# Attention rows staged in DRAM per batch: aligned 160-key loads, 32-row score matmuls, a values product by columns

## What is computed

```
# layer 0: a per-batch 32x32 mixing matrix, then 8 experts (hidden 128), the best 2 of 8 for each row
x = x + experts0(einsum('bct,bcd->bdt', x, w[conditions]))

# layer 1: paged attention with a window of 128 keys, 8 query heads over 4 key/value groups of 32
q, k, v = project(x); q, k = rope(rms(q)), rope(rms(k))
k_blocks[blk, :, off, :] = k        # the 32 new rows of each batch go into blocks of 16 rows
v_blocks[blk, :, off, :] = v        # (tables of different batches share blocks)
k_all, v_all = k_blocks[block_tables], v_blocks[block_tables]
scores = q @ k_all * SCALE, masked to  pos - 128 < kpos <= pos
o = softmax(scores) @ v_all @ Wo

# then 2 experts (hidden 1024), the best 1 of 2 for each row
x = x + experts1(o)
```

## Time and profile before

| | us |
|---|---|
| median of 3 runs | 1221.78 (1213.56 to 1230.88) |
| the profiled execution | 1226.37 |
| its span, first to last instruction | 1224.6 |
| PE busy | 945.7 (77%) |
| DVE busy | 721.4 (59%) |
| POOL busy | 559.1 (46%) |
| ACT busy | 535.9 (44%) |

### The profile page before, as it was taken

The page is one execution under the profiler, slowest core; times in us unless marked ns, Lnnn a source line. Parts: engine busy times, 40 slices in busy tenths (PEclk is TensorE's granted clock), DMA queues, the critical chain, the costliest instruction groups (busy, mean ns, idle before and its releaser), DMA issues.

```text
span 1224.6 us, 21749 instructions
## 1 busy us (share of the span) xinstructions
PE 945.7 (77%) x4475; PEld 698.1 (57%) x4476; DVE 721.4 (59%) x2742; ACT 535.9 (44%) x1733; POOL 559.1 (46%) x558
## 2 busy tenths in 40 slices
PE   1896600789993766639988888888886999999995
PEld 1895400556662322218866677666774666767664
DVE  4225670344443899968978788878884444444442
ACT  0231000122221433329978787878783433333331
POOL 0001775050003777546777777777762122222221
PEclk9999999999997988968999999999997999999998
DMA  6766224874336644312222222222221111111110
GB/s 167 272 209 178 106 102 173 314 232 130 120 119 242 182 139 141 107 45 66 68 69 73 63 70 73 67 70 70 70 75 47 38 51 52 48 47 43 50 36 26
DMA packets 93174, 130.04 MB, mean 106 GB/s; under 512 B 28729, under 2 KB 77419, under 8 KB 91808
## 3 DMA queue, kind: packets, MB, share of 16 engines
q0 software_dynamic: 33872, 68.94, 18.9%
q1 hardware_dynamic: 44688, 42.02, 10.8%
q10 hardware_dynamic: 14576, 18.65, 5.0%
HBM read 98.37 MB, written 55.38 MB: 126 GB/s over the span
## 4 chain that ended last, share of the span: by engine, by line
PE 42%; issue 19%; POOL 19%; DMA 9%; DVE 8%; DVEq 1%; ACT 1%; SPq 0%; POOLq 0%; ACTq 0%
POOL kvring L417 12%; PE bank L839 9%; PE bank L851 9%; POOL slots_in L421 7%; PE bank L723 6%; PE bank L652 3%; DMA kvring<-written_blocks,read_i 2%; DMA work<-in_x 2%; PE bank L715 2%; PE bank L860 2%; PE bank L663 2%; DMA work<-slots_in 1%; DVE work L1153 1%; PE bank L731 1%; PE bank L770 1%
## 5 line engine op out<-in xcount | busy, mean ns | idle before, releaser
L421 POOL DMA_INDIRECT slots_in<-rows,slot_i x96 | 98.6, 1027 | 152.0 <-DVE slot_i L980 102.9
L417 POOL DMA_INDIRECT kvring<-in_cache,read_i x128 | 137.4, 1073 | 49.9 <-issue 36.0
L417 POOL DMA_INDIRECT kvring<-written_blocks,read_i x128 | 137.9, 1077 | 41.4 <-issue 40.8
L770 PE MATMUL bank<-work,kvring 88*128 88x256 f32 x512 | 136.0, 388 | 0.9 <-issue 0.8
L417 POOL DMA_INDIRECT work<-slots_out,slot_i x64 | 72.4, 1132 | 126.7 <-DMA slots_out<-work 102.4
L839 PE MATMUL bank<-experts,work 128*128 x264 | 126.4, 601 | 0.6 <-ACT work L621 0.6
L851 PE MATMUL bank<-experts,work 128*128 x528 | 124.9, 379 | 1.8 <-DVE work L1252 1.8
L851 PEld LDWEIGHTS bank<-experts,work 128*128 128x128 f32 x528 | 100.1, 190 | 43.2 <-issue 32.9
L421 POOL DMA_INDIRECT out_x<-work x33 | 33.2, 1007 | 191.2 <-DVE work L1264 178.4
L582 ACT ACTIVATE work<-work 128x176 f32<-128x176 f32 x256 | 110.3, 433 | 7.3 <-DVE work L1205 5.6
L1247 DVE TENSOR_TENSOR work<-bank,work 128x512 f32<-128x512 f32 x66 | 45.7, 692 | 106.4 <-ACT work L629 106.4
(11 more groups left out here) (235 smaller groups left out, 2016.2 us busy)
## 6 DMA issues: line engine op xcount, KB each, us to landing
slots_in<-work ACTq DMA_DIRECT2D x8, 1152.0 KB, 5.1
work<-slots_in SPq DMA_DIRECT2D x72, 128.0 KB, 2.1
slots_out<-work SPq DMA_DIRECT2D x72, 128.0 KB, 1.7
work<-in_x SPq DMA_DIRECT2D x64, 128.0 KB, 2.4
written_blocks<-kvring POOLq DMA_DIRECT2D x3, 2048.0 KB, 7.6
slots_in<-fill ACTq DMA_DIRECT2D x1, 4257.0 KB, 17.6
work<-slots_in SPq DMA_DIRECT2D x33, 129.0 KB, 2.6
x_rows<-work SPq DMA_DIRECT2D x32, 128.0 KB, 2.5
```

The source lines that it names most:

```text
L417: pool.indirect_dma_start(dst, None, src, bass.IndirectOffsetOnAxis(ap=index, axis=0), **kw).then_inc(done, 16)
L421: pool.indirect_dma_start(dst, bass.IndirectOffsetOnAxis(ap=index, axis=0), src, None, **kw).then_inc(done, 16)
L770: mm = pe.matmul(bank[6 + q // 2 % 2][:, (q % 2) * 256:(q % 2) * 256 + 256], kv[q][:, r * 256 + KW:r * 256 + 2 * KW], pt[q % 2][:, r * 256 ...
```

## The change

A DRAM buffer `kv_rows` (16 units of 8 batches, 8 x 176 rows each) holds for each batch its 11 blocks in order. POOL fills it in two rounds: in stages 2 and 3 with blocks of the cache (a gather of 88 blocks of 16 KB into SBUF, then a scatter of them to DRAM, for each unit), and from the start of attention with overwritten blocks over them. The block numbers for that go from DVE's `blocks_i` to DRAM by four DMAs of POOL, and come back turned, by four DMAs of SP, as `read_i`. In attention SP reads the batch's first row offset (0 to 15) into a register and loads exactly NK = 160 keys from there with one plain DMA into one of GB = 8 buffers. The mask becomes the same shape for all batches, but for keys before the start. Scores are multiplied by group: four matmuls with 32 rows contracted (partitions 32g on), 64 columns held and 160 keys streamed, into two banks. The values product has eight matmuls, 80 rows contracted, 32 columns held, 64 streamed, each writing its own 32 partitions. Queries come by one POOL copy for each tile, and the copy of the turned probabilities moves from DVE to ACT, that of the keys from ACT to DVE.

```diff
 @@ SP, between stage 1 and stage 2
+            sp.wait_ge(s4_list, 64)
+            for w in range(4):
+                sp.dma_start(read_i[:, w * NU:w * NU + NU], block_list[w].rearrange("(u c) -> c u", u=NU),
+                             allow_slow_non_contiguous=True).then_inc(s4_index, 16)
             sp.wait_ge(s_sc0, 16 * 2 * NT)
 @@ SP, attention
+            stage3_drained(sp)
+            for b in range(B):
+                u, j = b // GB, b % GB
+                if j == 0:
+                    sp.wait_ge(s4_rows[u % 2], 16 * (NU // 2 + u // 2 + 1))
+                wait(sp, s4_pv, b - GB + 1)
+                first = nc.s_assert_within(sp.value_load(first_i[0:1, b:b + 1]), 0, BLK - 1,
+                sp.dma_start(kv[j], kv_rows[u][bass.ds(first + j * ROWS_B, NK), :].rearrange(
+                    "(k r) f -> k (r f)", r=2)).then_inc(s4_in[j], 16)
 @@ POOL, after the block copies
             pool.wait_ge(s_idx, 1)
-            for b in range(RING):
-                gather(kv[b], cache_pairs, read_i[:, b:b + 1], s4_in[b], NPHYS * 8 - 1)
+            for w in range(4):
+                pool.dma_start(block_list[w].rearrange("(b k) -> b k", b=B), blocks_i[:, w * NR:w * NR + NR]).then_inc(s4_list, 16)
+            pool.wait_ge(s4_index, 64)
+            for u in range(PRE2 + 1):
+                if u < PRE2:
+                    wait(pool, s2_d, u * N0 // (PRE2 + 1))
+                    stage_cache(u)
+                if u:
+                    write_rows(u - 1)
 @@ POOL, stage 3, for each tile i
+                    u, phase = PRE2 + i // 4, i % 4
+                    if u < NU and phase == 0:
+                        stage_cache(u)
+                    if u < NU and phase == 3:
+                        write_rows(u)
 @@ POOL, attention
-                    gather(kv[b % RING], cache_pairs, read_i[:, b:b + 1], s4_in[b % RING], NPHYS * 8 - 1)
-                gather(kv[c0 % RING], copies_pairs, read_i[:, B + c0:B + c0 + 1], s4_in[c0 % RING], NE * B * 8 - 1)
+            stage_copies(0)
+            for tile in range(2):
+                queries(tile)
+            write_copies(0)
+            stage_copies(1)
+            write_copies(1)
+            for s in range(B + 16):
+                u, tile = s // GB + 2, s // BT + 1
+                if s % GB == 0 and u < NU:
+                    stage_copies(u)
+                if s % GB == 3 and u < NU:
+                    write_copies(u)
+                if s % BT == 0 and 2 <= tile < NT:
+                    queries(tile)
 @@ PE, attention: scores
-                        mm = pe.matmul(bank[2 + q % 2][:, g * NK:g * NK + NK],
-                                       qbd[q // 4 % 2][:, (q % 4) * 256 + g * P:(q % 4) * 256 + g * P + P], kt[q % 2],
+                    for g in range(G):
+                        p0 = HD * g
+                        mm = pe.matmul(sbank[set_][g // 2][64 * (g % 2):64 * (g % 2) + 64, 0:NK],
+                                       qb[t][p0:p0 + HD, q % 4 * 64:q % 4 * 64 + 64],
+                                       kt[q // 2 % 2][p0:p0 + HD, (q % 2) * NK:(q % 2) * NK + NK], start=True, stop=True)
 @@ PE, attention: values
-                        mm = pe.matmul(bank[6 + q // 2 % 2][:, (q % 2) * 256:(q % 2) * 256 + 256],
-                                       kv[q][:, r * 256 + KW:r * 256 + 2 * KW], pt[q % 2][:, r * 256:r * 256 + 256],
+                        for g in range(G):
+                            p0 = HD * g
+                            mm = pe.matmul(vbank[t][p0:p0 + HD, 0:D].rearrange("p (h b t) -> p b h t", h=2, b=BT)[:, q % 4, :, :],
+                                           kv[q][:, r * 256 + KW + p0:r * 256 + KW + p0 + HD],
+                                           pt[q % 2][:, r * 256 + 64 * g:r * 256 + 64 * g + 64], start=(r == 0), stop=(r == 1))
 @@ ACT, attention (DVE loses its copy of the turned probabilities)
+                    act.activation(pt[q], tbank[0:KR, :], ACT.Copy).then_inc(s4_tpc, 1)
+                    act.activation(ot[t], vbank[t][:, 0:D], ACT.Copy).then_inc(s4_oc, 1)
+                    act.activation(col(rows, tile * RW, D), vbank[t][:, D:2 * D], ACT.Copy).then_inc(s4_wc, 1)
                         act.activation(pr[q][:, g * NK:g * NK + NK], sc[q][:, g * NK:g * NK + NK], ACT.Exp,
-                    act.activation(kt[q], bank[q][:, 0:NK], ACT.Copy).then_inc(s4_ktc, 1)
-                    act.activation(dist[q], c("keypos"), ACT.Abs, bias=col(delta, st.s + 2)).then_inc(s4_di, 1)
```

368 lines of the change are left out of this document (182 added, 186 removed).

## The result

The changed kernel took 1617.26 us (median of 4 runs, 1614.03 to 1622.21), the kernel before 1223.66 beside it: a ratio of 1.323, with a 95% interval of 1.313 to 1.333. The forecast was 1295 with a range to 1380. The side was right, and the size was missed by more than 300 us.

What follows compares the result with a forecast made beforehand. The prediction took POOL to bound attention before, PE stage 2, and POOL's cycle the middle of stage 3. It summed +57 + 18 + 10 - 12 = +73 on 1226.4 us, less 4.6, to 1295 us, range 1210 to 1380.

Steps and rivals of the forecast that it cites:

- POOL never rests: Attention before: POOL's instructions and issue gaps fill 324 of 325 us, a pace of 2.92 us a batch.
- Part 1: Way to stage 2: SP's first load waits for POOL's stores, at 265 us (250 to 275); +57 us (+40 to +80).
- POOL pays some 12 us of the same kind: Stage 2: 16 transfers of 1.44 MB running through it cost some 12 us, within the +57.
- Part 2: Stage 3: 16 more transfers in POOL's list ahead of gathers DVE waits on; +18 us (+5 to +60).
- four buffers hide that, or they don't: Stage 3: later landing of small gathers and scatters is hidden by four buffers, or costs 16 x 2 to 4 us.
- Part 3: Attention's start: gather, scatter and load follow each other, 15 us in place of 4; +10 us (+5 to +16).
- Part 4: Attention's batch: 2.83 us against 2.92 by columns streamed, -12 us over 128 batches; chance 0.42.
- PE sets the batch: Attention: PE's passes sum to 2.83 us a batch, against 2.0 each for ACT and DVE.
- lands in 2.5 us: Attention: SP's load of 160 keys takes some 2.5 us, hidden while a batch takes over 2.2 us.
- Rival 1: Attention: passes on strips run beside each other, about 2.4 us a batch, -67 us, total 1240 us; chance 0.27.
- the round trip decides: Within Rival 1: scores, masks, exponentials, copy, then values take some 2.8 us, giving about 2.4 us a batch.
- Rival 3: Attention: short passes cost more than their columns, batch 3.23 to 3.63 us, total 1347 to 1398 us; chance 0.23.

Runs made afterwards that it cites:

- e17: e13 unchanged, run again together with e16; 1235.92 us, ratio 1.016 to the kernel before.
- e5: e3 with the masking of scores moved first in each step of DVE's attention loop; 1357.87 us.
- e1: Changed kernel with only two of 16 units filled in the first (cache) round, so most batches read another batch's keys; 1490.14 us.
- e4: Changed kernel with scores and values multiplied in whole-array forms, including products nobody asked for; 1612.84 us.
- e11: Changed kernel with the mask first on DVE and scores and values in e4's whole-array forms, output not attention's result; 1617.85 us.
- e2: Changed kernel with the four loads of block numbers issued by POOL and not SP; 1586.44 us.
- the combined kernel: The kernel of e10, all four repairs on the changed kernel; 1297.22 us as it was, 1271.9 us with 96 rows (e18).
- e15: e10 with `PRE2 = 16`, so the whole first round lies beside stage 2; 1339.8 us where the kernel before took 1320.49.
- e6: e3 with one more matmul per batch into an unused part of a bank, read by nobody; 1504.8 us.
- e3: Changed kernel without the second round of transfers (overwritten blocks), so rows this call writes are missing from the keys; 1500.05 us.
- e13: Kernel before with its own gathers of pairs (176 keys), no DRAM buffer, and the changed kernel's attention, mask first; 1377.38 us, ratio 1.045.
- e18: e10 with block transfers of 96 rows instead of 88, the extra rows outside the bounds; 1271.9 us, ratio 0.960 to the kernel before.
- e10: Changed kernel with mask first, overwritten blocks left out of the first round, block numbers loaded by POOL, and 16 key buffers; 1297.22 us, ratio 1.073.
- e16: The kernel before, unchanged, profiled on the chip on which e17 runs; 1221.92 us.

## Why the prediction was wrong, by its steps

**"POOL never rests" before: right.** e17 shows it: another attention behind the same gathers gives nearly the same pace, 2.98 us a batch for 2.92. e5 shows that there was room under it, 354 us against 399.5, though without the copies round.

**Part 1, the first load of stage 2: right.** 256.2 us, where 250 to 275 was given; the loads of `read_i` took 3.45 us on SP and stand where the prediction put them:

```profile
252.72 3.45 SPq L391 DMA_DIRECT2D read_i<-blocks_by_batch  x4
256.22 4.49 SPq L397 DMA_DIRECT2D work<-slots_in  x6
```

**Part 1, "POOL pays some 12 us of the same kind" in stage 2: wrong.** The 12 us were set by what six copies of 128 rows cost stage 2 before; parts 2 and 3 took these copies' window rate, 342 GB/s, for transfers of 88 rows. But these take 13 to 15 us each for 1.44 MB, so that 16 of them are there for nearly all of stage 2. Stage 2 took 60 us more, of which e1 gave back 53. The term of +57 measured +107.

**Part 2, stage 3 at +18 (+5 to +60): undersized.** It measured +74. The price of POOL's instructions was right. What failed is "four buffers hide that, or they don't", which was left without working out who waits: ACT does, 99.8 us, for buffers whose scatters land after 12.2 us in place of 2.4. This is the same wrong transfer time, a second time.

**Part 3, +10: measured +22,** the first unit's gather landed after 10.1 us and its scatter after 9.6, in place of 5.9 each (1.3 and 4.6), and the first load took 3.2.

**Part 4, the batch at 2.83 us: wrong, and the largest error.** It measured 4.39, +190 us in place of -12. Two steps failed. First, "PE sets the batch": passes on separate strips do run beside each other, so PE needed less than the 2.83 us (it was busy 2.3 us a batch in e5, at a clock of 0.85), and what set the batch was the loop through all engines' lists in their order. The forecast looked at each engine's sum, 2.0 for ACT and for DVE, and never at what stands ahead of the mask in DVE's list. Second, the SP load "lands in 2.5 us" and is hidden "while a batch takes over 2.2 us": the price of a load alone, while the copies round was known to run beside it. Of the changed kernel's 128 loads, the 76 that met a block transfer took 6.1 us in the median and up to 11.7, and they were asked for one batch and 1.1 us ahead.

**Rival 1: its mechanism was right,** and its 2.4 us a batch is near what e5 showed once both limits were gone (2.55), though with the rows of the copies round left out. The place where it said "the round trip decides" was the right question; it counted only the trip's own durations and not the instructions that stand between them in each list. **Rival 3** named a batch of 3.2 to 3.6 us, from a cause that isn't there: on strips the short passes overlap, and 16 of them took 0.43 us in e5, less than their columns' price of 0.85. The Trainium skill ("TensorEngine Tiling (Array Packing)", Key Properties) says that a change of the tiling mode drains the array. No run here prices that: e4 and e11, without strips, took 1613 and 1618 us, but both with late keys, where PE's time was hidden.

Of the 393 us, then: 47 are SP's list (e2 gave 31 of them back), 126 the first round's transfers beside stages 2 and 3, 22 the first transfers of the second round, and 190 attention, where the order on DVE and the late keys stand in one loop. The other 8 are small differences, nearly all in stage 2 with the two units of e1.

## What to carry to other kernels

When a change writes new lists for several engines, follow one item through all of them and write down what stands ahead of it in each list; the sum of each engine says nothing of that. When two waits lie on one loop, an experiment that mends only one of them can show almost nothing; try each with the other out of the way (the mask's place gave 12 us, and then 90 to 139). After a repair ask what it took away: 16 key buffers cost a staging buffer, and that then set the pace. And take the time of a transfer from a row of the same shape and count of partitions, then ask who waits for the small transfers beside it.

## What the runs showed of the hardware

- Float32 matmuls on strips run beside each other. Two rows of e5's timeline, PE alone:

```profile
901.72 0.50 PE L831 MATMUL bank<-work 32*64 32x160 f32 x8
...
903.49 0.43 PE L862 MATMUL bank<-work 80*32 80x64 f32 x16
```

  Eight passes of 160 keys take 0.50 us, where full-array passes of 176 columns stand 0.147 apart and eight would take 1.2; sixteen passes of 64 columns take 0.43 us, where the forecast had 0.85. In the same trace the four strips' passes start 7 ns apart (901.717 to 901.737 us, and four value passes from 903.488 to 903.508). The Trainium skill ("TensorE: Matmul & The Clock Gate", Part 3: Packing small matmuls) states such overlap; these runs agree, for float32. The forecast wrote that this overlap was measured with other types, but that section names none.
- Indirect transfers of 88 rows of 16 KB took 13.0 us (1.44 MB, e1), while 128 rows (2.1 MB) landed in 7 to 8. With 96 rows in the index, and no byte more, the combined kernel stood at 0.960 of the kernel before, where e15 (with `PRE2 = 16`) stood at 1.015. That the count of rows sets how many DMA engines share a transfer is what the packet records suggest (11 to 13 packets in flight, then 15 to 17); only the gain is measured.
- PE's granted clock was 0.97 in the kernel before's attention (nearly all of the time at the upper of its levels, 1.2 and 2.4 GHz) and 0.59 after, with PE busy 69% of the time in short passes. It rose with a filler (0.65 to 0.79, e6 beside e3) or with whole-array forms (0.78, e4), without any gain in time. With the mask first it rose to 0.85 and the time fell (e5): there the clock followed the shorter waits.
- A load that meets a larger transfer waits with it. 160 KB took 2.2 us with no block transfer beside it and 6.1 in the median, up to 11.7, with one (the changed kernel). In stage 3 the small scatters into `written_blocks` took 12.2 us in place of 2.4.
- Beside e13 to e15 and beside e18 the kernel before took 1320 us, 8% more than beside the others. One kernel's attention took 408 us in e17 and 521 in e13, while with the DRAM buffer it took 410 in e10 and 407 in e15. So it is the attention with POOL's gathers of pairs that was longer there. POOL's 302 instructions were busy the same time in both (300.5 and 303.0 us), and why was not tried. Whether it is the chip is open too: e13 and e16 are on record with the same chip number.
